# A pairwise-interaction tower on one core: units of one tile with column pieces of 128 in place of row pieces alone

## The reference

```python
e = jnp.stack([tbl_f[ids[:, f]] for f in range(32)], axis=1)   # 1024 x 32 x 64
left = jnp.einsum('bpd,pde->bpe', e[:, idx_i, :], W)           # 496 pairs
z = jnp.sum(left * e[:, idx_j, :], axis=-1)
h = jnp.concatenate([z, dense_ctx], axis=1)                    # 1024 x 512
h = jnp.maximum(h @ W_top1 + b_top1, 0.0)                      # 512
h = jnp.maximum(h @ W_top2 + b_top2, 0.0)                      # 256
y = h @ W_top3
```

## Time and profile before

| | |
|---|---|
| median of 3 runs | 444.05 us |
| profiled execution | 444.54 us, span 442.6 us |
| TensorE busy | 383.9 us, 87% (2384 records) |
| VectorE busy | 367.3 us, 83% (403) |
| ScalarE busy | 351.7 us, 79% |
| GpSimd busy | 325.2 us, 73% |
| granted TensorE clock, mean | 0.973 |

### The profile page before, as it was taken

How to read it: one execution, slowest core, us unless ns; L and a number is a source line. 1 busy time by engine, 2 the same in 40 slices (tenths; PEclk the granted TensorE clock), 3 DMA queues, 4 the chain that set the end, 5 groups by cost and what they waited for, 6 DMA issues and landing times. The chain is left out here.

```text
span 442.6 us, 9364 instructions
## 1 busy us (share of the span) xinstructions
PE 383.9 (87%) x2384; PEld 208.7 (47%) x2384; DVE 367.3 (83%) x403; ACT 351.7 (79%) x2719; POOL 325.2 (73%) x448
## 2 busy tenths in 40 slices
PE   0368767799999999999899979989999999698978
PEld 0223333545554545555555534555455535334557
DVE  0029979899999899999789996988989898889980
ACT  1199979949999987869697986995879677879972
POOL 5776777777777777778787787887878778885620
PEclk9999889999999999999999998999999999989997
DMA  6999991111122211111111111111111111000000
GB/s 125 170 165 161 161 165 27 27 28 27 29 48 68 49 27 23 22 21 23 20 22 21 20 22 24 20 21 21 22 22 21 21 21 20 19 2 0 3 0 2
DMA packets 44703, 18.91 MB, mean 43 GB/s; under 512 B 39781, under 2 KB 40298, under 8 KB 44650
## 3 DMA queue, kind: packets, MB, share of 16 engines
q1 hardware_dynamic: 36138, 8.86, 15.8%
q0 software_dynamic: 8512, 9.45, 11.1%
HBM read 18.29 MB, written 0.00 MB: 41 GB/s over the span
## 5 line engine op out<-in xcount | busy, mean ns | idle before, releaser
L870 ACT ACTIVATE row_products<-row_products 128x64 f32<-128x64 f32 x1312 | 313.6, 245 | 9.0 <-DVE row_products L799 7.4
L730 POOL DMA_INDIRECT rows<-in_tbl_dram,ids_sb x256 | 243.1, 950 | 85.7 <-POOL pause L724 33.6
L870 ACT ACTIVATION_READ_ACCUMULATOR row_products<-row_products 128x1 f32 x1312 | 251.6, 192 | 0.0
L799 DVE TENSOR_TENSOR row_products<-left,rows 128x1024 f32<-128x1024 f32 x120 | 144.4, 1217 | 19.6 <-PE left L979 19.1
L979 PE MATMUL left<-w_sb,X 64*128 64x512 f32 x480 | 130.4, 634 | 9.7 <-DVE row_products L799 4.2
L789 DVE TENSOR_TENSOR column_products<-left,X 128x1024 f32<-128x1024 f32 x78 | 93.7, 1216 | 12.2 <-PE left L974 12.2
L974 PE MATMUL left<-X,w_sb 64*128 64x256 f32 x720 | 97.2, 395 | 1.7 <-ACT X L854 1.2
L974 PEld LDWEIGHTS left<-X,w_sb 64*128 64x128 f32 x720 | 67.7, 190 | 41.8 <-issue 17.8
L979 PEld LDWEIGHTS left<-w_sb,X 64*128 64x128 f32 x480 | 43.1, 193 | 49.9 <-issue 18.6
L806 DVE TENSOR_TENSOR row_products<-left,rows 128x512 f32<-128x512 f32 (+2 forms) x56 | 37.8, 721 | 26.4 <-PE left L984 25.5
L854 ACT ACTIVATE X<-turned 128x512 f32<-128x512 f32 (+2 forms) x43 | 20.6, 478 | 42.9 <-PE turned L937 42.9
(11 more groups left out here) (38 smaller groups left out, 148.4 us busy)
## 6 DMA issues: line engine op xcount, KB each, us to landing
rows<-in_tbl_dram,ids_sb POOLq DMA_INDIRECT x256, 2.5
w_sb<-in_W_top_dram SPq DMA_DIRECT2D x1, 512.0 KB
w_sb<-in_L_rec_W_dram SPq DMA_DIRECT2D x1, 496.0 KB, 12.3
w_sb<-in_L_rec_W_dram SPq DMA_DIRECT2D x1, 480.0 KB, 11.9
w_sb<-in_L_rec_W_dram SPq DMA_DIRECT2D x1, 464.0 KB
w_sb<-in_L_rec_W_dram SPq DMA_DIRECT2D x1, 448.0 KB
w_sb<-in_L_rec_W_dram SPq DMA_DIRECT2D x1, 432.0 KB
w_sb<-in_L_rec_W_dram SPq DMA_DIRECT2D x1, 416.0 KB
```

The costliest lines, as they stand in the source:

```text
L730: pool.indirect_dma_start(out=rows[:, u % 2 * QT + t, f * D:(f + 1) * D], out_offset=None, in_=tables[f], in_offset=bass.IndirectOffsetOnA ...
L799: ins = nc.vector.tensor_tensor(to, of, fields[:, :, 2 * D * c:2 * D * (c + 4)].to_broadcast([P, 2, BANK]), ALU.mult)
L870: ins = nc.scalar.activation(product, product, ACT.Copy, accum_out=to)
```

## The change

A unit of one tile is cut into the same kinds as a wide one: 15 rows, 30 columns and 2 own pieces. Column and own pieces there stream 128 samples in place of 256, so that they have 512 outputs per partition in two half banks; the reductions have 256 columns. The rest and neighbours pieces and their code go. There are then 280 pieces, 120 of them with a row sum (before 152), and 320 reductions. z_sum is copied for every unit. The planner gets a price for a narrow multiply, new values of its other constants, and a rule that holds back the last turn of reductions of a unit until the unit before it has come far enough in the MLP. PAUSES, AHEAD, RING and the batches stay.

```diff
-X_WAIT, MLP_WAIT = 16, 12
+X_WAIT, MLP_WAIT = 18, 12
-WORK, OWN, SUM, SET, TRANSPOSE, LAYER, SWITCH, RELOAD = 0.85, 1.85, 0.23, 0.15, 0.12, 1.72, 0.1, 0.12
-MULTIPLY, ROWSUM_DVE, ROWSUM_ACT, ROWSUM_POOL, COPY, RELU, SIGNAL = 1.23, 1.3, 4.0, 4.4, 0.6, 0.47, 0.12
-GATHER_FIRST, GATHER, LANDING, W_FIRST, W_PAIR = 3.5, 1.25, 6.0, 6.0, 0.1
-ACT_SLACK, DVE_SLACK, MARGIN, NEAR, POOL_AFTER = 0.5, 1.0, 0.1, 0.3, 2
+NARROW, WORK, OWN, SUM, SET, TRANSPOSE, LAYER, SWITCH, RELOAD = 0.69, 0.85, 1.85, 0.2, 0.15, 0.12, 1.72, 0.1, 0.12
+MULTIPLY, ROWSUM_DVE, ROWSUM_ACT, ROWSUM_POOL, COPY, RELU, SIGNAL = 1.26, 1.23, 3.9, 4.8, 0.6, 0.47, 0.12
+GATHER_FIRST, GATHER, LANDING, W_FIRST, W_PAIR = 3.5, 1.25, 5, 6.0, 0.1
+ACT_SLACK, DVE_SLACK, MARGIN, NEAR, POOL_AFTER = 1, 0.8, 0.1, 0.3, 0
...
-    for u, (_, n) in enumerate(UNITS):
-        if n == QT:
-            columns += [("own", u, slot) if isinstance(slot, int) else ("columns", u, slot) for slot in SLOTS]
-        pieces = [("rows", u, t, m, c) for m, c in ROW_UNITS for t in range(n)]
-        if n < QT:
-            pieces += [("rest", u, 0, slots) for slots in REST] + [("neighbours", u, 0)]
-        rows += sorted(pieces, key=lambda x: -least_field(x))
+    for u in range(len(UNITS)):
+        columns += [("own", u, slot) if isinstance(slot, int) else ("columns", u, slot) for slot in SLOTS]
+        rows += [("rows", u, t, m, c) for m, c in ROW_UNITS for t in range(tiles(u))]
...
+        if i and self.sums % SUMS == SUMS - TURN and (self.mlp, self.stage) < (i - 1, 5):
+
+            return None
...
-        self.on_pe("sum", begin, TURN * SUM)
+        self.on_pe("sum", begin, TURN * SUM * tiles(self.sums // SUMS) / QT)
...
-        length = {"own": OWN, "neighbours": 2 * OWN}.get(x[0], WORK)
+        share = 1 if by_rows(x) else tiles(x[1]) / QT
+        length = (OWN if x[0] == "own" else WORK) * share
...
-        plan.insert(plan.index(("work", first - 4 + 2 * n)), ("wT", n))
+        plan.insert(plan.index(("work", first - 3)), ("wT", n))
...
+                    a, c = columns_before[w], columns_of(q)
+                    to, of = [bank[:, :, 0:2 * c].rearrange("p o (g b) -> p o g b", b=c)
+                              for bank in (column_products[:, a % COLUMN_PRODS, :, :], left[:, s, :, :])]
...
+                    fields = X[:, n:n + 1 + (k2 != k), 0:c].unsqueeze(1).to_broadcast([P, 2, 2, c])
+                    nc.vector.tensor_tensor(to, of, fields, ALU.mult).then_inc(multiplied, 1)
...
+                width = columns_of(q)
                 if x[0] == "columns":
                     for g, (m, k) in enumerate(x[2]):
                         for odd in (0, 1):
-                            ins = nc.tensor.matmul(left[:, s, odd, QB * g:QB * (g + 1)], weights(odd, m, k, 2),
-                                                   X[D * odd:D * odd + D, q % 2 * FP + m, :], start=True, stop=True)
+                            ins = nc.tensor.matmul(left[:, s, odd, width * g:width * (g + 1)], weights(odd, m, k, 2),
+                                                   X[D * odd:D * odd + D, q % 2 * FP + m, 0:width], start=True, stop=True)
...
-                nc.tensor.matmul(z_sum[32 * r:32 * r + 32, :], ones_window[:, 30 - 2 * t:62 - 2 * t],
-                                 column_products[:, v // 2 % COLUMN_PRODS, v % 2, :],
+                nc.tensor.matmul(z_sum[32 * r:32 * r + 32, 0:2 * width], ones_window[:, 30 - 2 * t:62 - 2 * t],
+                                 column_products[:, v // 2 % COLUMN_PRODS, v % 2, 0:2 * width],
```

More of the change, by code:

```diff
@@ L24 @@
 LAST = len(UNITS) - 1
-WIDE = [u for u, (_, n) in enumerate(UNITS) if n == QT]
 NPAIR = F * (F - 1) // 2
@@ L194, in first_gather @@
     return 2 * FP * UNITS[u][0] + 2 * tiles(u) * (FP - 1 - m)
-WITHIN = [sum(x[1] == 0 and least_field(x) >= FP - n for x in make_work()[1]) for n in range(FP + 1)]
+WITHIN = [sum(x[1] == 0 and least_field(x) >= FP - n for pieces in make_work() for x in pieces) for n in range(FP + 1)]
 def pieces_before(g):
@@ L339, in sum_rows @@
                 self.by_act(self.waiting.pop(0))
-            elif gathered is not None and self.rows[self.waiting[0]][0] == "rows" and max(self.pool, gathered - POOL_AFTER, ready) <= now + ACT_SLACK:
+            elif gathered is not None and max(self.pool, gathered - POOL_AFTER, ready) <= now + ACT_SLACK:
                 self.by_pool(self.waiting.pop(0))
@@ L521, in make_plan @@
     for n in (0, 1):
-        first = next(w for w, x in enumerate(order.work) if x[0] == "neighbours" or x[0] == "own" and x[2] == 8 - 8 * n)
-        plan.insert(plan.index(("work", first - 4 + 2 * n)), ("wT", n))
+        first = next(w for w, x in enumerate(order.work) if x[0] == "own" and x[2] == 8 - 8 * n)
+        plan.insert(plan.index(("work", first - 3)), ("wT", n))
     return plan, order.work, order.batches
@@ L653, in columns_of @@
             return P * tiles(u)
[L655 to L661, removed]
         block = ctx.enter_context(nc.Block())
@@ L795, in multiply @@
                     wait_row_sums(dve, n - ROW_PRODS + 1)
[L796 to L812, removed]
@@ L819, in row_sum @@
                 z_nat_free(dve, x[1])
[L820 to L825, removed]
-                    by_chunk = z_nat[:, 2 * b, :].rearrange("p (c r) -> p c r", c=2)
-                    for o in (0, 1):
-                        for i in (0, 1):
-                            _, row = z_place(x, o, 4 * i)
-                            four = products[:, o, 4 * D * i:4 * D * (i + 1)]
-                            if x[0] == "rest":
-                                to, of = by_chunk[:, :, row:row + 2], four.rearrange("p (c r d) -> p c r d", c=2, d=D)
-                            else:
-                                to, of = by_chunk[:, :, row:row + 33:32], four.rearrange("p (r c d) -> p c r d", c=2, d=D)
-                            ins = nc.vector.tensor_reduce(to, of, AX.X, ALU.add)
@@ L953, in transpose_z @@
                 for c in (0, 1):
-                    for t in (0, 1):
-                        column, tile, half = (QB * c + P * t, t, c) if tiles(q) == QT else (QB * c + P * t, c, t)
-                        ins = nc.tensor.transpose(turned[:, column:column + P], z_nat[:, q % 2 * QT + tile, P * half:P * half + P], ident[:, :])
+                    for t in range(tiles(q)):
+                        column = columns_of(q) * c + P * t
+                        ins = nc.tensor.transpose(turned[:, column:column + P], z_nat[:, q % 2 * QT + t, P * c:P * c + P], ident[:, :])
                 ins.then_inc(transposed, 1)
@@ L967, in project @@
                 if q == 0:
-                    for m in {"columns": lambda: [m for m, k in x[2]], "rows": lambda: [x[3]], "own": lambda: range(x[2], x[2] + 8),
-                              "rest": lambda: [m for _, m, k, n in runs(x)], "neighbours": lambda: range(FP)}[x[0]]():
+                    for m in [m for m, k in x[2]] if x[0] == "columns" else [x[3]] if x[0] == "rows" else range(x[2], x[2] + 8):
                         pe.wait_ge(w_loaded[m], 32 if m < FP - 1 else 16)
+                width = columns_of(q)
                 if x[0] == "columns":
@@ L980, in project @@
                                                weights(odd, m, c, 8), start=True, stop=True)
-                elif x[0] == "rest":
-                    for place, m, k, n in runs(x):
-                        for odd in (0, 1):
-                            ins = nc.tensor.matmul(left[:, s, odd, P * place:P * (place + n)], X[D * odd:D * odd + D, q % 2 * FP + m, 0:P],
-                                                   weights(odd, m, k, 2 * n), start=True, stop=True)
-                elif x[0] == "neighbours":
-                    pe.wait_ge(copied, max(copies["wT", 0], copies["wT", 1]))
-                    for m in range(FP):
-                        o, part = m % 2, slice(m % 2 * D, m % 2 * D + D)
-                        ins = nc.tensor.matmul(left[:, s, o, m // 2 * D:(m // 2 + 1) * D], X[part, q % 2 * FP + m, 0:P],
-                                               w_sb[part, w_base(m) + 1, :], start=True, stop=True)
                 else:
```

92 lines of the change are left out of this document (32 added, 60 removed).

## The result

The changed kernel takes 436.49 us in the median (436.25 to 437.63, 4 runs), against 443.54 us before on the same occasions (441.13 to 444.2, 4 runs). The ratio is 0.986, 95% interval 0.981 to 0.990. The profiled execution took 437.63 us with a span of 435.8, so 6.8 us of the span of 442.6 are gone; 8 were forecast.

What follows compares the result with a forecast made beforehand. VectorE was taken to bound one-tile units after the first window, TensorE nearly full in wide ones. Terms -4 (64.3 to 176.8), -1.5 (last unit), -1 and -1.5 (end) sum to -8: 444.54 to 436.5 us, range 430 to 443.

Steps and rivals of the forecast that it cites:

- signs of being wrong: PE spaces narrow pieces at 0.6 or more; unit 1 does not end before 173 us; units 2 and 3 each change over 3 us.
- Prices: Work per engine, both small units: narrow PE piece 0.43 us (bounds 0.43, 0.86); VectorE -25 us, TensorE +15.8 us.
- rival A: Slower: narrow pieces cost PE more than half, a loss from 0.62 us a piece; 446 to 456 us, chance 0.28.
- The last unit: Window 373.8 to 430 us: VectorE falls to 40, PE at 52 becomes the bound; -1.5 us.
- The tail: After the last multiply: shorter chain of sums -1 us, layer 1 of the last unit at a higher clock -1.5 us.
- 64.3 to 176.8: -4 us: In this window VectorE falls to 97 us and PE reaches 101, giving 108.6 us: -4 us.
- units 2 and 3: 0: The wide units are PE-bound before and after the change, so their time does not change: 0.
- it needs none to be ahead of unit 4: The last gather, moving forward up to 10 us, needs no forward move to precede unit 4.
- PE-bound: In wide units TensorE's demand is 90.3 us against 99.6 and 97.4 measured, 91 and 93%: nearly full.
- Most of those waits vanish: In the gather stream, waits for multiplies mostly go, so the last gather moves forward by up to 10 us.
- rival C: Much faster: PE is not the bound, VectorE's saving counts but for 4 us; 418 to 429 us, chance 0.15.
- What the planner does: 0, bounds -3 and +3: In wide units the planner's new prices and waits were taken as 0 us, bounds -3 and +3.

Runs made afterwards that it cites:

- doubled runs: Changed kernel, order unchanged: each narrow column matmul issued twice, 450.69 us; or each narrow column multiply done twice, 449.29 us.
- the order chosen anew: Kernel before, old pieces and memsets kept, with planner constants picked among many replayed orders of work: 445.09 us, ratio 1.008.
- the replay: Orders replayed with trace durations to pick constants, memsets kept: kernel before with its pick 445.09 us, changed kernel with its pick 437.14 us.

## Why the prediction was right, and where it was not

The number came true, 436.5 forecast and 436.49 measured, and the prices of the sum are right. The way to it is right in the last unit and wrong in the middle. Two of the prediction's own signs of being wrong came: unit 1 ends at 176.5 us and not before 173, and units 2 and 3 change by -10.3 and +6.2 us, more than 3 each.

- **Prices, right.** A narrow piece on PE: 0.45 us, forecast 0.43 with bounds 0.43 and 0.86. Counted with the change of kind it is 0.50 to 0.54, still under rival A's 0.62, from which the change would lose. The Trainium skill ("TensorE: Matmul & The Clock Gate", section "Back-to-back issue gap") has 81 ns for 128 columns in a stream of load and matmul pairs, against 56 by its formula: the rise to 1.45 times that the prediction estimated from it does not show in a run of these fp32 pieces. VectorE's busy time fell from 367.3 to 339.1 us, by 28 (forecast 25). As taken, ScalarE made no more sums than before.
- **The last unit, right in kind.** VectorE 42.0 busy us (forecast 40), PE full, the window 1.6 us shorter (forecast 1.5), though from piece end to piece end it is 0.4. With unit 4 alone narrow VectorE fell as far and the window did not get shorter, and doubling TensorE's work made it 11 us longer with PE full: PE took over. Doubling VectorE's costs 11 us as well, so VectorE stands closer behind than I had it.
- **The tail, right in sum.** From the last multiply to the end it was 14.2 us (428.4 to 442.6) and is 12.2 (423.6 to 435.8); forecast -2.5, measured -2.0. Layer 1 gave 2.8 instead of 1.5. The higher clock there is no effect of the pieces: with the old pieces layer 1 also took 3.81 us under the new constants, in the order chosen anew and without memsets, and with the new pieces 5.58 under the old constants. The shorter chain of sums gave nothing: from the last multiply to layer 1 it is 3.8 us, before 3.0, for unit 3's layer 3 and the reductions now stand there.
- **"64.3 to 176.8: -4 us" and "units 2 and 3: 0", wrong in place.** After was 10.6 us ahead at the end of unit 2 and 4.4 at the end of unit 3. The step that failed is the one on the gathers, "it needs none to be ahead of unit 4". It compared the last gather with the last unit and never asked of unit 3, whose transposes stand in PE's order against rows that come every 1.67 us. The doubled runs price that in the changed kernel at nearly 8 us of unit 3, and in the kernel before the run with the memsets gone prices it at 8 of the 441.34 us measured beside it. My reading that wide units are "PE-bound" at 91 and 93% took this waiting for PE's own limit; without the memsets they take 93.6 and 94.3 us with the same work, near the 90.3 of the sum.
- **"Most of those waits vanish", wrong.** The last gather was to move forward by up to 10 us, as its waits for multiplies went. It moved by 1.8. With TensorE's narrow work doubled it starts at 381.2 us as in after, though the multiplies of units 2 and 3 come 10 us later: the multiplies did not hold the gathers. Most follow each other by 1.60 us and one in four by 1.88, which is the 1.67 in the mean. The 374 us on which rival C counted were out of reach for the same reason.
- **"What the planner does: 0, bounds -3 and +3", wrong.** The constants alone (with the old pieces the new rule too) are worth +2.9 us with the old pieces (446.31 against 443.39) and -12.7 with the new. The gain of the change is that of pieces and order together. Of the pieces alone no run gives one value: +6 us, -10, -8 with three pairs of orders, and +3 without memsets (434.86 against 431.88). That the sum came out right to 0.1 us is chance: -4 forecast for 64.3 to 176.8 and 0 for units 2 and 3 stand against -4.4 at the end of unit 3, reached by another way.
- **Rival C**, VectorE's saving in full: fell with the doubled runs, where TensorE had not the room that it needs.

What stays open is which single places of the order cost most of the 12.7 us, why the changed kernel gained only 1.6 us without the memsets when its waits for rows were gone, and why the replay missed by 5 us.

## What to carry to other kernels

When work moves from one nearly full engine to another, price both, and then look for the input whose pace did not change: time gained ahead of a paced stream is handed back where the order next meets it. A statically ordered kernel should be compared with its order refitted on both sides, since here the order was worth more (12.7 us) than the change (7 us). A pitch that the planner counts as 1.6 us and the chip runs at 1.67 in the mean adds up to 9 us over 128 gathers; read such constants back from the trace.

## What the runs showed that was not expected

- A pacing memset of 0.38 us ahead of each gather cost the kernel before 8 us, with nothing else changed (ratio 0.982, 0.978 to 0.986).
- A wait of 2.46 us of PE was paid twice: behind it the granted clock was at the 1.2 GHz level for a while (0.60 in the mean from 265.9 to 269.1), and the 16 records of the reductions took 3.09 us instead of 1.92.
- For fp32, 128 columns per weight load ran as fast on PE as 256: 0.45 us for half of the 0.86 us piece.
